# First attention: the context's turns of two batches ahead, issued ahead of the first two heads' scores

## The chip, the cores and the metric

The kernel runs on one core of one Trainium2 chip. The metric is device microseconds of one execution, the median of several runs. In the profile PE is TensorE (matrix products and transposes), PEld its weight loads, DVE is VectorE, ACT is ScalarE, POOL is GpSimd and SP is the engine that issues most DMAs. Each engine runs its own list of instructions strictly in order; engines meet only at semaphores.

## The reference, cut to what matters

The network has four layers, each an attention over a context and a mixture of experts, with gated residuals. Data are float32: x is 16 batches x 100 tokens x 256, the context 16 x 361 x 192. The change is in the first layer's attention, which per batch computes

```
xn = layernorm(ctx, ln_x_g, ln_x_b)                   # 361 x 192
ln = layernorm(layernorm(x), ln_l_g, ln_l_b)          # 100 x 256
q  = ln @ Wq.T
k, v = concat([xn @ Wkv.T, ln @ Wlkv.T], axis=1) split in two
q, k normalized by their root mean square per head (4 heads of 64)
attn = softmax(mask(q @ k.T)) ; out = (attn @ v) @ Wo.T + bo
x = x + tanh(g_xattn[0]) * out
```

so the keys are 361 of the context and 100 of the tokens, padded to 512 columns. Expert layers and three more attentions follow and are the same in both kernels.

## The kernel before, in words

The program is written engine by engine, its order by hand, with counting semaphores. The first attention treats one batch t at a time and works on three batches at once: while batch t is attended, the projections of t + 1 are finished and those of t + 2 begun. `three_deep` (line 218) runs batches 0 to 3 unrolled, 4 to 11 as two rounds of a loop of four, and 12 to 15 unrolled.

Each batch has twelve numbered steps on TensorE, each filling one of two banks of PSUM in turn (`J_bank`), which another engine empties; a step may begin when the step before the last has been copied out (line 2370 or 2344: `wait_for(pe, s.copied, order_of(t, n) - 1)`). The steps in their order are `AHEAD = (0, 1, 5, 6, 2, 8, 3, 4, 9, 10, 7, 11)`:

- 0 and 1, `ctx_turn` (line 2379): three 128 x 128 transposes each of the normalized context of batch t + 2; ScalarE copies each out with gain and bias (line 1067) into CT.
- 5 and 6, then 7 and 11, in pairs: the projections of the context to keys and values. 192 rows of contraction are taken as 128 (`pair_blocks`, line 2352) and 64 (`pair_rests`, line 2360); the two rests of a pair use the two halves of TensorE's rows. ScalarE squares and copies the results out (lines 1075 to 1077, 1079, 1080, 1082).
- 2, 3 and 4: the turn of the tokens (line 2396, copied at line 1071), queries, and keys and values of the tokens (both line 2402).
- 8, 9 and 10: the turns of the normalized keys and queries of batch t + 1 (lines 2419 and 2422), copied out by ScalarE (lines 1087 and 1089).

TensorE's attention proper: `scores` (line 2468, two heads at a time, each in one half of the rows, into banks 0 and 1), `probs_turn` (line 2479), `weigh` (line 2500), `o_turn` (line 2509, with a transpose for the router, line 2281) and `project` (line 2519). VectorE adds the mask to the scores and takes the maximum (line 1605), negates it (line 1609) and copies turned probabilities out (line 1620). ScalarE takes the exponential (line 1112), which waits for the maximum.

VectorE's order within a batch (line 1750): maxima of heads 0 and 1; a sum of squares for t + 1; statistics of the context and tokens of t + 3; probabilities of heads 0 and 1; the context's norm; maxima of heads 2 and 3; residual, router, sums of squares for t + 2; probabilities of heads 2 and 3; the scaling of the output. ScalarE's order (line 1180): copies of steps 7 and 11 of t + 1; copies of steps 0 and 1 of t + 2; exponentials of heads 0 and 1; the copy of the output; copies of 5, 6 and 2; exponentials of heads 2 and 3; copies of 8, 3, 4, 9 and 10.

On TensorE the bank of step 0 of batch t + 2 was last filled by step 7 of batch t + 1, that of step 1 by step 11; both come from the rests that open the batch:

Of the kernel before, what the change touches and what calls it, by code (L numbers as in the profile page):

```python
# [136 lines left out]
def order_of(t, n):  # L137

    if n not in OF_NEXT:
        return ALONE.index(n) if isinstance(t, int) and t == 0 else 9 + 12 * (t - 1) + AHEAD.index(n)  # L140
    return 9 + 12 * t + (n - 8 if isinstance(t, int) and t == B - 1 else AHEAD.index(n))
# [24 lines left out]
def copied_by(L, t):  # L166

    return STEPS[L] if L == 1 and isinstance(t, int) and t == 0 else VALUE_PAIRS[L][-1][0]
# [7 lines left out]
def follows(t, by):  # L176

    return not isinstance(t, int) or t + by < B
# [7 lines left out]
def wait_for(eng, signal, count):  # L186

    if isinstance(count, int) and count <= 0:
        return
    eng.wait_ge(signal.sem, signal.before + count)  # L190
# [48 lines left out]
def flamingo_kernel(nc, a, out):  # L239
    ctx = ExitStack()  # L240
    with ctx:
# [313 lines left out]
        def kt(L, j):  # L555
            m = 4 if L == 1 else 2
            return KT[j][:, 0:m * 512].rearrange("p (m n) -> p m n", m=m)
# [1716 lines left out]
        def _(pe):  # L2274
# [31 lines left out]
            def attention(L):  # L2306
# [11 lines left out]
                def part_of(t, j, n, r, rest):  # L2318

                    c = 1 - r if rest else r  # L2320
                    lo, hi = (REST * c, REST * (c + 1)) if rest else (0, P)
                    if L == 0:
                        keys = (r if n in FIRST_PAIRS[0] else 2) * P
                        cols = slice(0, 512) if n in FIRST_PAIRS[0] else slice(D * r, D * (r + 1))
                        return ((J_bank[parity_of(t, n)][:, 0:cols.stop - cols.start], CT[j][lo:hi, c, keys:keys + P],
                                 wkv0[lo:hi, c, cols]),)
                    dst = step_bank(L, t, j, n)
                    if n in sum(KEY_PAIRS[L], ()):
                        m = sum(KEY_PAIRS[L], ()).index(n)
                        return ((dst[:, 0:NC], wk[L][lo:hi, c, m * P:(m + 1) * P], CT[j][lo:hi, c, 0:NC]),)  # L2330
                    last = CT[j][lo:hi, c, 2 * P:3 * P]
                    if L == 1 and n >= 8:
                        return ((dst[:, 0:256], last, wv[1][lo:hi, c, 256 * r:256 * (r + 1)]),)
                    whole = (dst[:, 0:VN], CT[j][lo:hi, c, r * P:(r + 1) * P], wv[L][lo:hi, c, 0:VN])
                    if L == 1:
                        return (whole,)
                    return (whole, (dst[:, 256:384], last, wv[2][lo:hi, c, P * r:P * (r + 1)]))

                def pair_blocks(t, j, pair):

                    for r, n in enumerate(pair):
                        if L == 0:

                            wait_for(pe, s.copied, order_of(t, n) - 1)
                            if n == 5:
                                wait_for(pe, s.copied, order_of(t, 1) + 1)
                        else:
                            wait_for(pe, s.copied, STEPS[L] * t + place_of(L, t, n) - 1)
                            if n == KEY_PAIRS[L][0][0]:
                                wait_for(pe, (s.ctx_in0, s.ctx_in1)[j], 32 * (t // 2 + 1))  # L2350
                        for i, (to, lhs, rhs) in enumerate(part_of(t, j, n, r, False)):
                            nc.tensor.matmul(to, lhs, rhs, start=(i == 0), stop=False, skip_group_check=True)  # L2352

                def pair_rests(t, j, pair):

                    parts = [part_of(t, j, n, r, True) for r, n in enumerate(pair)]
                    for i in range(len(parts[0])):
                        for r in range(2):
                            to, lhs, rhs = parts[r][i]
                            ins = nc.tensor.matmul(to, lhs, rhs, start=False, stop=True, skip_group_check=True)  # L2360
                            if i == len(parts[0]) - 1:
                                ins.then_inc(s.proj.sem, 1)
# [82 lines left out]
                def scores(t, j, h):  # L2445
                    n = H * t + h
                    k = (H * j + h) % 2

                    if PAIRS[L] == 0:
                        wait_for(pe, s.exped, n - 1)  # L2450
                    elif h % 2 == 0:
                        wait_for(pe, s.exped, n)
                    if h == 0 and L == 0:

                        wait_for(pe, s.copied, order_of(t, 10) + 1)
                    elif h == 0 and L == 3:

                        wait_for(pe, s.copied, STEPS[L] * (t + 1))
                    elif h == 0:

                        wait_for(pe, s.copied, STEPS[L] * t + copied_by(L, t))
                    if H == 1:
                        for c, m in ((0, CW[0]), (1, CW[1] + 1)):
                            ins = nc.tensor.matmul(S_bank[k][0:T, 0:NK], QT[j][0:m, c, :], CT[j][0:m, c, 0:NK],
                                                   start=(c == 0), stop=(c == 1))
                    else:
                        m, b = h // 2, W * (h % 2)
                        ins = nc.tensor.matmul(S_bank[k][0:T, 0:NK], QT[j][b:b + W, m, :], kt(L, j)[b:b + W, m, 0:NK],  # L2468
                                               start=True, stop=True)
                    ins.then_inc(s.scores.sem, 1)  # L2470
# [32 lines left out]
                def o_turn(t, j, slot=0):  # L2503

                    wait_for(pe, s.o_scaled, 2 * (t + 1))
                    wait_for(pe, s.resid, 2 * t)
                    for m in range(H * W // P):
                        n, lo = (CW[m], m * HALF) if L == 3 else (P, m * P)
                        ins = nc.tensor.transpose(R_bank[0:n, m * T:(m + 1) * T], O[0:T, lo:lo + n], ident[0:T, 0:T])
                    if L == 0 and not (isinstance(t, int) and t == 0):  # L2510
                        ins = router_turn(t - 1, slot)
                    ins.then_inc(s.o_turned.sem, 1)
# [93 lines left out]
                def ahead(t, q, steps):  # L2606

                    for n in steps:
                        if n not in OF_NEXT and follows(t, 2):
                            step(t + 2, (q + 2) % 4, n)  # L2610
                        if n in OF_NEXT and follows(t, 1):
                            step(t + 1, (q + 1) % 4, n)

                def first_attend(t, q):
                    j = q % 2
                    started = not (isinstance(t, int) and t == 0)
                    if follows(t, 1):
                        pair_rests(t + 1, 1 - j, FIRST_PAIRS[1])
                    scores(t, j, 0)
                    scores(t, j, 1)  # L2620
                    ahead(t, q, (0, 1))
                    if started:
                        o_turn(t - 1, 1 - j, (q + 2) % RING)
                    if follows(t, 2):
                        pair_blocks(t + 2, j, FIRST_PAIRS[0])
                    probs_turn(t, j, 0)
                    probs_turn(t, j, 1)
                    if follows(t, 2):
                        pair_rests(t + 2, j, FIRST_PAIRS[0])
                    scores(t, j, 2)  # L2630
                    scores(t, j, 3)
                    if started:
                        project(t - 1, 1 - j)
                    ahead(t, q, (2,))
                    weigh(t, q, 0)
                    weigh(t, q, 1)
                    ahead(t, q, (8, 3, 4, 9, 10))
                    if follows(t, 2):
                        pair_blocks(t + 2, j, FIRST_PAIRS[1])
                    probs_turn(t, j, 2)  # L2640
                    probs_turn(t, j, 3)
                    weigh(t, q, 2)
                    weigh(t, q, 3)
# [487 lines left out]
```

## Time and profile before

| | |
|---|---|
| runs | 1673.85, 1675.27, 1681.13 us; median 1675.27 |
| profiled execution | 1673.62 us, span 1671.4 us |
| busy, share of the span | PE 91%, PEld 66%, DVE 54%, ACT 36%, POOL 17% |
| first attention, batch 7 (182.7 to 202.8 us) | PE 18.17, DVE 15.60, ACT 10.78, POOL 11.52 us |
| granted TensorE clock, mean | 0.952 |

A batch is taken here from the start of its first scores to that of the next batch's. Times of the timeline count from the start of the span. A row gives the start, the time taken, engine, line, operation, output and input with their shapes and the number of instructions merged into it; what stands in brackets at its end is the idle time of the engine before it and what ended that. An engine's consecutive rows can overlap by some tenths of a microsecond, since a new instruction enters before the last is out. A float32 matrix product shows as two records, a transpose as one.

### The profile page before, as it was taken

How to read it: one execution, taken by the hardware profiler on the slowest of the kernel's cores; microseconds unless marked ns; L12 is line 12 of the kernel's file. 1: busy time of each engine (PE TensorE's matmuls, PEld its weight loads, DVE VectorE, ACT ScalarE, POOL GpSimd, SP SyncE). 2: the span in 40 equal slices, each digit the busy share in tenths (PEclk: the TensorE clock that was granted, in tenths of full speed). 3: DMA queues.
4: the chain of work that ended last, by engine and by line, in shares of the span. 5: the costliest groups of instructions: out<-in, count | busy, mean ns of one | idle time of the engine just before them, and what ended most of it. 6: DMA issues, size and time to landing. Idle time of an engine off the chain costs nothing.

```text
span 1671.4 us, 30315 instructions
## 1 busy us (share of the span) xinstructions
PE 1515.2 (91%) x9070; PEld 1100.3 (66%) x9070; DVE 900.9 (54%) x2901; ACT 607.6 (36%) x1705; POOL 291.3 (17%) x409
## 2 busy tenths in 40 slices
PE   5889889878999989999999989979999899787986
PEld 2555555557999966777677666747777644565664
DVE  4678787652222224555444444556665555565665
ACT  3555555512333223344443424314444100444422
POOL 4555555411000031000000000110000011121000
PEclk8999999958999989999999989989999799999888
DMA  5011112618999940000000000011010100342000
GB/s 135 16 45 37 36 34 62 200 44 281 332 327 327 330 151 22 19 18 18 18 15 11 9 1 10 16 41 37 27 35 18 32 16 19 85 149 66 1 20 20
DMA packets 89654, 128.85 MB, mean 77 GB/s; under 512 B 17362, under 2 KB 74786, under 8 KB 84450
## 3 DMA queue, kind: packets, MB, share of 16 engines
q1 hardware_dynamic: 85954, 123.50, 22.9%
q0 software_dynamic: 2432, 4.34, 0.8%
q8 instruction: 39, 0.64, 0.2%
q14 instruction: 45, 0.37, 0.1%
q10 hardware_dynamic: 1184, 0.01, 0.0%
HBM read 112.87 MB, written 11.67 MB: 75 GB/s over the span
## 4 chain that ended last, share of the span: by engine, by line
PE 70%; issue 10%; DVE 8%; POOL 6%; ACT 3%; DMA 1%; POOLq 0%; ACTq 0%; SPq 0%; DVEq 0%
PE bank L2352 9%; PE bank L2706 8%; PE bank L2500 8%; PE bank L2799 5%; PE bank L2360 5%; PE bank L2468 4%; PE bank L2720 4%; PE bank L2519 4%; PE bank L2752 3%; PE bank L2479 3%; PE bank L2768 3%; PE bank L2441 2%; POOL work L922 2%; PE bank L2952 2%; DVE work L1620 1%
## 5 line engine op out<-in xcount | busy, mean ns | idle before, releaser
L1620 DVE COPY work<-bank 128x300 f32<-128x300 f32 (+1 forms) x272 | 123.2, 490 | 178.6 <-PE bank L2479 177.3
L2500 PE MATMUL bank<-work 128*100 128x64 f32 (+1 forms) x1760 | 193.7, 261 | 19.3 <-DVE work L1620 17.4
L2500 PEld LDWEIGHTS bank<-work 128*100 128x100 f32 x1760 | 175.2, 171 | 47.5 <-DVE work L1620 28.3
L1112 ACT ACTIVATE work<-bank,work 100x361 f32<-100x361 f32 (+1 forms) x272 | 158.7, 590 | 49.4 <-DVE work L1611 34.8
L2706 PE MATMUL bank<-work 128*128 128x128 f32 x1216 | 142.2, 275 | 0.0
L1955 DVE SCALAR_TENSOR_TENSOR work<-bank,work 128x128 f32<-128x128 f32 x160 | 56.2, 351 | 158.9 <-PE bank L2706 148.1
L2706 PEld LDWEIGHTS bank<-work 128*128 128x128 f32 x1216 | 140.4, 192 | 1.0
L1611 DVE TENSOR_REDUCE work<-bank 100x1 f32<-100x361 f32 x208 | 101.9, 528 | 69.3 <-PE bank L2468 66.7
L2479 PEld LDWEIGHTS bank<-ident,work 100*128 100x128 f32 x880 | 92.1, 144 | 42.1 <-issue 22.7
L2479 PE MATMUL bank<-ident,work 100*128 100x100 f32 x880 | 103.9, 254 | 7.3 <-ACT work L1112 7.0
L1233 ACT ACTIVATE work<-bank,work 128x128 f32<-128x128 f32 x160 | 58.7, 367 | 142.2 <-PE bank L2706 137.2
L2468 PE MATMUL bank<-work 64*100 64x361 f32 (+1 forms) x512 | 109.0, 503 | 0.6 <-ACT work L1096 0.6
L1102 ACT COPY work<-bank 128x512 f32<-128x512 f32 (+2 forms) x96 | 41.3, 482 | 166.5 <-PE bank L2360 166.5
L900 POOL TENSOR_TENSOR work<-work,neg_half 100x1 f32<-100x1 f32 x64 | 35.2, 550 | 340.1 <-DVE work L1569 305.3
L922 POOL TENSOR_TENSOR work<-work,neg_half 128x4 f32<-128x4 f32 x80 | 82.0, 1025 | 65.1 <-DVE work L1593 65.1
L2799 PE MATMUL bank<-F_weight,work 128*128 128x512 f32 (+1 forms) x208 | 92.4, 603 | 0.0
L859 POOL TENSOR_TENSOR work<-work,neg_half 100x1 f32<-100x1 f32 x48 | 28.1, 586 | 296.5 <-DVE work L1477 271.0
L1099 ACT COPY work<-bank 128x361 f32<-128x361 f32 x96 | 39.6, 465 | 94.6 <-PE bank L2360 94.6
L2720 PE MATMUL bank<-work 128*128 128x256 f32 x320 | 72.5, 380 | 0.5 <-DVE work L1955 0.5
L2799 PEld LDWEIGHTS bank<-F_weight,work 128*128 128x128 f32 (+1 forms) x208 | 39.1, 190 | 49.2 <-issue 39.8
L2352 PE MATMUL bank<-L_WkvT,work 128*128 128x512 f32 (+1 forms) x128 | 52.9, 536 | 17.3 <-ACT work L1067 13.8
L2720 PEld LDWEIGHTS bank<-work 128*128 128x128 f32 x320 | 59.3, 190 | 7.9 <-DVE work L1955 0.7
(343 smaller groups left out, 2770.4 us busy)
## 6 DMA issues: line engine op xcount, KB each, us to landing
work<-in_F_w SPq DMA_DIRECT2D x58, 1024.0 KB, 5.8
work<-in_ctxT SPq DMA_DIRECT2D x64, 180.5 KB, 2.3
work<-context_norms SPq DMA_DIRECT2D x32, 288.0 KB, 3.4
context_norms<-work SPq DMA_DIRECT2D x16, 288.0 KB, 2.5
work<-in_ctx SPq DMA_DIRECT2D x16, 192.0 KB, 2.6
work<-in_F_b SPq DMA_DIRECT2D x20, 128.0 KB, 6.1
work<-sorted_x SPq DMA_DIRECT2D x20, 128.0 KB, 2.2
sorted_y<-work SPq DMA_DIRECT2D x20, 128.0 KB, 5.7
```

What stands on the lines that cost most here:

```text
L922: nc.gpsimd.tensor_tensor(rr[j][:, 4 * k:4 * k + 4], rr[j][:, 4 * k:4 * k + 4], neg_half[:, 0:4], ALU.pow).then_inc(s.rqk.sem, 1)
L1112: nc.scalar.activation(pr[:, 0:NK], S_bank[k][0:T, 0:NK], ACT.Exp, bias=nmax[k][0:T, :], accum_out=rsum[j][0:T, h:h + 1]).then_inc(s.exped ...
L1611: nc.vector.tensor_reduce(nmax[k][0:T, :], S_bank[k][0:T, 0:NK], axis=AXX, op=ALU.max, negate=True).then_inc(s.maxed.sem, 1)
L1620: nc.vector.tensor_copy(PT[k][:, 0:CH, :], PT_bank[k][:, 0:CH * T].rearrange("p (c t) -> p c t", c=CH)).then_inc(s.probs_copied.sem, 1)
L2352: nc.tensor.matmul(to, lhs, rhs, start=(i == 0), stop=False, skip_group_check=True)
L2360: ins = nc.tensor.matmul(to, lhs, rhs, start=False, stop=True, skip_group_check=True)
L2468: ins = nc.tensor.matmul(S_bank[k][0:T, 0:NK], QT[j][b:b + W, m, :], kt(L, j)[b:b + W, m, 0:NK], start=True, stop=True)
L2479: ins = nc.tensor.transpose(PT_bank[k][:, c * T:(c + 1) * T], PR[k][0:T, c, :], ident[0:T, 0:T])
L2500: ins = nc.tensor.matmul(to, PT[k][:, c, :], values, start=(c == 0), stop=(c == CH - 1))
L2706: ins = nc.tensor.matmul(bank[to + f % 2][:, 0:P], first_weights(i, j)[:, c, col:col + P], TT[j][:, c, :], start=(c == 0), stop=(c == 1))
L2720: ins = nc.tensor.matmul(bank[6 + j][:, 0:D], AC[j][:, f, :], W2[j][:, f, :], start=(f == 0), stop=(f == HID0 // P - 1))
L2799: ins = nc.tensor.matmul(bank[3 + q % Y_BANKS][0:k, :], GXT[:, c, i * P:i * P + k], lin2[:, c, 2 * g:2 * g + 2, :].rearrange("p e n -> p ( ...
```

## The change

In TensorE's list for the first attention, the call that issues steps 0 and 1 of batch t + 2 moves ahead of the scores of heads 0 and 1. It acts in batches 0 to 13; batches 14 and 15 have no batch two ahead. Other engines' lists, all waits and all operands stay.

```
@@ first_attend(t, q), TensorE
                     if follows(t, 1):
                         pair_rests(t + 1, 1 - j, FIRST_PAIRS[1])
+                    ahead(t, q, (0, 1))
                     scores(t, j, 0)
                     scores(t, j, 1)
-                    ahead(t, q, (0, 1))
                     if started:
                         o_turn(t - 1, 1 - j, (q + 2) % RING)
                     if follows(t, 2):
```

## Rows read from the trace of the kernel before

**Rows 1.** Busy time in stretches: window, length, busy us of each engine, clock, DMA
```profile
182.70:202.80 20.10, 18.17 (x116) 12.11 (x114) 15.60 (x62) 10.78 (x30) 11.52 (x15) 1.00 0.12 37
202.80:225.00 22.20, 18.57 (x116) 12.05 (x114) 15.98 (x62) 11.11 (x30) 9.92 (x13) 1.00 0.11 33
183.90:192.80 8.90, 8.25 (x54) 5.46 (x54) 8.37 (x30) 5.33 (x15) 3.79 (x5) 1.00 0.21 63
```

**Rows 2.** Waits, 50 to 300 us: who, for whom, total us, times, longest
```profile
PE bank L2352 <- ACT work L1067: 8.4, 12, 0.9
```

**Rows 3.** Timeline, TensorE, batch 7: start, us, line, work, idle before
```profile
182.16 0.70 PE L2360 MATMUL bank<-L_WkvT,work 64*128 64x256 f32 x4
182.69 1.02 PE L2468 MATMUL bank<-work 64*100 64x512 f32 x4
183.75 0.87 PE L2390 MATMUL bank<-ident,work 128*128 128x128 f32 x6
185.61 1.98 PE L2352 MATMUL bank<-L_WkvT,work 128*128 128x512 f32 x4 [0.65 <-ACT work L1067]
187.44 0.85 PE L2479 MATMUL bank<-ident,work 100*128 100x100 f32 x8
194.91 1.98 PE L2402 MATMUL bank<-L_WlkvT,work 128*128 128x512 f32 x4
202.80 1.02 PE L2468 MATMUL bank<-work 64*100 64x512 f32 x4
```

**Rows 4.** Timeline, ScalarE, batch 7
```profile
183.25 0.37 ACT L1080 COPY work<-bank 128x256 f32<-128x256 f32 x1
184.33 1.23 ACT L1067 ACTIVATE work<-bank,L_ln_x_b,L_ln_x_g 128x384 f32<-128x384 f32 x2 [0.43 <-PE bank L2390]
193.49 0.69 ACT L1112 ACTIVATE work<-bank,work 100x512 f32<-100x512 f32 x1
194.16 0.70 ACT L1087 ACTIVATE work<-bank,L_kn_g 128x512 f32<-128x512 f32 x1
```

**Rows 5.** Timeline, VectorE, batch 7
```profile
183.90 0.70 DVE L1605 CUSTOM_DVE_ANT_0 bank<-bank,work 100x512 f32<-100x512 f32 x1 [0.99 <-PE bank L2468]
192.63 0.15 DVE L1609 TENSOR_SCALAR work<-work 100x1 f32<-100x1 f32 x1
```

**Rows 6.** Timeline, batch 7: weight loads of the turns; rests behind transposes
```profile
183.74 0.64 PEld L2390 LDWEIGHTS bank<-ident,work 128*128 128x128 f32 x6 [0.88 <-issue]
188.22 1.13 PE L2360 MATMUL bank<-L_WkvT,work 64*128 64x512 f32 x4
```

**Rows 7.** Timeline, batch 8, which begins VectorE's second round of its loop
```profile
206.69 0.70 DVE L1605 CUSTOM_DVE_ANT_0 bank<-bank,work 100x512 f32<-100x512 f32 x1 [3.68 <-issue]
209.50 0.56 PE L2479 MATMUL bank<-ident,work 100*128 100x100 f32 x4 [0.29 <-ACT work L1112]
217.14 1.98 PE L2402 MATMUL bank<-L_WlkvT,work 128*128 128x512 f32 x4 [0.53 <-ACT work L1087]
```

**Rows 8.** Timeline, batches 0 and 3: fourth maximum's negation, exponential of head 3
```profile
54.05 0.15 DVE L1609 TENSOR_SCALAR work<-work 100x1 f32<-100x1 f32 x1
54.24 0.69 ACT L1112 ACTIVATE work<-bank,work 100x512 f32<-100x512 f32 x1
112.00 0.15 DVE L1609 TENSOR_SCALAR work<-work 100x1 f32<-100x1 f32 x1
113.10 0.69 ACT L1112 ACTIVATE work<-bank,work 100x512 f32<-100x512 f32 x1
```

**Rows 9.** Batch 14: busy time in a stretch; timeline of TensorE
```profile
325.00:345.00 20.00, 17.08 (x94) 12.38 (x92) 11.58 (x44) 6.52 (x16) 4.05 (x5) 0.74 0.04 10
328.36 0.56 PE L2479 MATMUL bank<-ident,work 100*128 100x100 f32 x4 [1.49 <-ACT work L1112]
329.27 0.56 PE L2479 MATMUL bank<-ident,work 100*128 100x100 f32 x4 [0.35 <-ACT work L1112]
329.76 1.47 PE L2468 MATMUL bank<-work 64*100 64x512 f32 x4
```

More of the change, by code:

```diff
@@ L2618, in first_attend @@
                         pair_rests(t + 1, 1 - j, FIRST_PAIRS[1])
+                    ahead(t, q, (0, 1))
                     scores(t, j, 0)
                     scores(t, j, 1)
-                    ahead(t, q, (0, 1))
                     if started:
```

## The prediction

> **What bounds the kernel now.** The change touches only the first attention (44 to 360 us of the span), so I read that stage: stretches of busy time first, then the waits, then one batch instruction by instruction on each engine. The reader is to see, first, that batch 7 takes 20.1 us, of which TensorE is busy 18.2, VectorE 15.6, ScalarE 10.8 and GpSimd 11.5, at the full clock [rows 1]. (The page's chain runs through GpSimd here and mostly says "issue"; an engine idle for half of the batch that waits on VectorE's results is no bound, so I don't follow it.) TensorE is the bound, with short stalls. One of them is the target: the blocks of keys (line 2352) wait for ScalarE's copies of the turned context (line 1067), 12 times between 50 and 300 us, 8.4 us in total [rows 2].
>
> Second, what TensorE does before that stall [rows 3]. The rests end at 182.86 (182.16 + 0.70), the two scores run from 182.69 to 183.71, the six turns start at 183.75 and take 0.87, the blocks start at 185.61 after 0.65 idle. The turns could not have started much earlier: the first goes into the bank that step 7 filled, and ScalarE's copy of it ends at 183.62 [rows 4]. The scores lie in exactly that hole.
>
> Third, and this decides for me: VectorE begins its batch with the maxima of those scores, at 183.90, and between 183.90 and 192.80 it is busy 8.37 of 8.90 us [rows 1, 5]. It has no slack from the first maximum to the fourth. Behind the fourth stand, on ScalarE, the exponentials of heads 2 and 3 and then the copy of step 8 (line 1087, ends 194.86), and TensorE's step 4 starts at 194.91, when that copy frees its bank [rows 3, 4].
>
> **The change part by part.** Nothing is added or removed: in each of batches 0 to 13 six transposes pass two score matmuls (batches 14 and 15 have no context two ahead). No DMA and no other engine's order changes; ScalarE already copies the turns before its exponentials. TensorE takes the waits along, so the scores, the turn of the output, the blocks and all behind now queue behind the turns' wait.
>
> (a) The turns' wait. The copy of step 7 ends at 183.62; from ScalarE's end to TensorE's start pass 0.05 (185.56 to 185.61) [rows 3, 4], so the turns start at 183.67 instead of 183.75 (the last three wait for step 11 in the same way, whose copy follows at once). TensorE, with nothing to do in between, idles 0.81 from the end of the rests. This is new cost, since its cover, the scores, is gone.
>
> (b) The scores. Turns until 183.67 + 0.87 = 184.54, scores 1.02, end 185.56 instead of 183.71: 1.85 us later. Bounds: 1.78 if the scores overlap the turns' tail by the 0.07 by which line 2360 overlaps the transposes before it, and 1.97 if they take the 1.13 which that row of four 512-column matmuls takes behind transposes [rows 6]; I take 1.85, which is between.
>
> (c) The stall at the blocks. The copies of the context come 0.08 earlier, but the scores and then 0.34 of turns of the output (184.62 to 184.96) stand first: the blocks start at 185.56 + 0.34 = 185.90, without a stall. The 0.65 is filled by 1.02 of scores, after a new hole of 0.81: TensorE alone loses 0.29 a batch.
>
> (d) What is late next on TensorE: the turn of the second head's probabilities. In the batch where VectorE started late, it began 2.81 us behind the first maximum (206.69 to 209.50) [rows 7]. With the maximum at 183.90 + 1.85 = 185.75 that is 188.56, against 187.44 + half of 0.85 = 187.87 now: 0.69 late, which contains the 0.29.
>
> (e) What is late next through VectorE: its first maximum is 1.85 late and nothing up to the fourth absorbs it. The only slack is ScalarE's: the fourth maximum's negation ends at 192.78, the exponential of head 3 starts at 193.49 although 0.04 would do: 0.67. So exponential, copy of step 8 and step 4 come 1.85 - 0.67 = 1.18 late, which contains the 0.69 of (d). Batch 8 is a trial of this: VectorE came back from its loop 2.68 us late (206.69 against 183.90 + 20.11, without any wait for another engine), and step 4 started at 217.14 instead of 194.91 + 20.11 = 215.02, 2.12 late [rows 3, 5, 7]: 0.56 absorbed, near the 0.67. Behind step 4 all waits up to the next rests are between TensorE and ScalarE and shift along, VectorE is idle 4.5 us in a batch, so it catches up before the next maxima. GpSimd gets its sums 1.85 later; it is idle 8.6 of 20.1 [rows 1].
>
> (f) The sum. ScalarE's slack, read as in (e) for each batch, is 0 in batch 0, 0.18, 0.50 and 0.91 in batches 1 to 3, 0.48, 0.60, 0.59, 0.67 in 4 to 7, 0.58, 0.59, 0.67 in 9 to 11, 0.86 in 12 and 1.25 in 13 (two of the pairs in [rows 8]). Batches 0 to 3: 7.40 - 1.59 = 5.8. Batches 4 to 7 and 9 to 11: 12.95 - 4.18 = 8.8. Batch 12: 1.0. Batch 13: 0.7, by (d), since its slack leaves less. Batch 8: 0, for there VectorE's return (206.69) is later than the new scores (202.80 + 1.02 + 1.85 + the 0.19 from scores to maximum = 205.86). Sum: +16.3 us. The next stage starts behind the last batch and shifts whole. The profiled execution took 1673.62 (span 1671.4); with the sum 1689.9. The median of the runs is 1.65 higher, so 1690 to 1691.5.
>
> A rule that speaks against the change: loading of the turns' weights starts only at 183.74, 0.88 after the loads before, when the half-row scores are through; but in the other direction, line 2360 starts at once behind the transposes [rows 6]. The Trainium skill, TensorEngine Tiling (Array Packing), Key Properties, says that changing the tiling mode drains the engine. The change makes one change of mode per batch (rests and scores to turns) into three. By the row a drain shows no gap in a matmul's start, so I add 0; by the page two more drains a batch would be charged, which makes the kernel slower still.
>
> **The rivals.**
> 1. *TensorE's loss only.* VectorE's delay is absorbed ahead of step 4. Then the loss is the 0.29 of (c) to the 0.69 of (d), in 12 batches (0 and 8 have longer stalls there): 3.5 to 8.3 us, about 1680. For it: VectorE does have 4.5 us idle in a batch. Against it: none of that lies between the first and fourth maximum, and batch 8 handed on 2.12 of 2.68.
> 2. *The stall goes, and little takes its place: faster.* If TensorE is the only bound and the turns' new wait is under 0.65, the two scores fill the old stall. It decides at a hole of 0.65 between rests and turns; with half of my 0.81 the gain is 0.25 in 13 batches, 3 us: 1672; with none 8.5 us, 1667. It needs ScalarE to copy step 7 sooner, and that copy starts from the rests, which don't move; and it needs VectorE not to matter.
> 3. *The clock falls.* In batch 14, after idling 1.49 before a turn of probabilities and 0.35 before the next, TensorE's granted clock fell, 0.74 on average from 325 to 345, and two scores then took 1.47 instead of 1.02 [rows 9]. The Trainium skill, TensorE: Matmul & The Clock Gate, Part 1, says that throttled is the default and activity releases it. The change makes stalls of 0.81, some 0.3 and 0.5 a batch. Against it: batch 8 with 18.57 busy of 22.2 stayed at 1.00 [rows 1], as much as I expect of the changed batches. At half clock two scores cost 0.45 more; a dip in every batch over both pairs of scores and as much work again costs some 2 us each (an estimate from these rows), 26 us on top of my sum, 1716; a few dips give 1695.
>
> That the change doesn't do what it says is excluded: the order on TensorE is written by hand, and the bank's wait moves along.
>
> **How the numbers follow.** My forecast 0.74, rival 1 0.14, rival 2 0.05, rival 3 0.07. Time 1690. The forecast's own range comes from (b), 1.78 to 1.97 in 12 batches (-1 to +1.4), ScalarE's slack off by 0.15 each (2 us) and the runs' spread: 1685 to 1696. The range takes in the upper part of rival 1 and the small dips of rival 3: 1681 to 1697. 0.5% is 8.4 us, about what a measurement can tell from no change: rival 1 lies within it but for its top, rival 2 also, but for its end near 1667. Faster 0.03, same 0.15, slower 0.82.
>
> **What would show it.** Right: the turns start some 0.05 after the end of line 1080, with TensorE idle 0.8 before them; no stall before line 2352; the first maximum 2.9 after the end of the rests instead of 1.04; step 4 waiting for line 1087 in every batch; batches of 21.3 us, and batch 8 near 22.2 as before. Wrong: batches of 20.4 to 20.8 would say that VectorE's delay is absorbed (rival 1), a hole under 0.65 rival 2, a granted clock under 1 before 325 us rival 3.

## The result, and the profile after

The changed kernel is slower. Over the first four executions its median is 1696.18 us (1687.33 to 1697.98) against 1674.91 before (1673.85 to 1681.13): a ratio of 1.0109, 95% interval 1.0066 to 1.0152. Five more rounds on another occasion gave 1.0102 (1.0072 to 1.0131). The forecast was 1690, range 1681 to 1697. The profiled execution of the changed kernel took 1697.98 us, span 1695.8, mean granted clock 0.952 as before.

First the stage as a whole. A mark that both kernels pass in the same way is ScalarE's square of step 7 (line 1079), 0.11 us behind the rests that open a batch. In the timeline of the kernel before, its first row is that of batch 0 and its second that of batch 14:

```profile
44.65 0.38 ACT L1079 ACTIVATE work<-bank 128x256 f32<-128x256 f32 x1 [1.42 <-PE bank L2360]
...
325.54 0.38 ACT L1079 ACTIVATE work<-bank 128x256 f32<-128x256 f32 x1 [4.16 <-PE bank L2360]
```

That is 280.89 us for 14 batches; in the changed kernel it is 342.63 - 44.76 = 297.87 (first and last row of the second fence below). So the stage is 16.98 us longer; the sum had said 16.3.

Busy time in stretches of the changed kernel, with the columns of [rows 1]: batch 7, batch 8, from the first to the fourth maximum of batch 7, and the 20 us with the least TensorE work of the stage.

```profile
192.70:214.06 21.36, 18.60 (x114) 11.90 (x114) 15.49 (x61) 11.09 (x30) 11.41 (x16) 1.00 0.12 35
214.07:236.82 22.75, 18.69 (x114) 11.89 (x114) 16.00 (x61) 11.12 (x30) 10.66 (x14) 1.00 0.12 32
195.56:204.45 8.89, 8.69 (x59) 5.71 (x58) 8.35 (x30) 5.21 (x15) 3.03 (x4) 1.00 0.05 13
205.00:225.00 20.00, 15.97 (x90) 9.30 (x89) 12.89 (x51) 9.06 (x26) 11.22 (x14) 1.00 0.13 37
```

Batch 7 takes 21.36 us instead of 20.1, with the busy time of every engine unchanged within 0.5 us [rows 1]: TensorE idles 0.83 us more and is busy 0.43 more, most of which is scores of 1.10 instead of 1.02 and eight transposes in two groups (0.56 and 0.57) instead of one run of 0.85. VectorE is again busy 8.35 of 8.89 us between first and fourth maximum. The clock stays at 1.00, also where TensorE is busy only 15.97 of 20.

The timeline of the changed kernel, all engines, batch 7 with marks of batches 0, 8 and 14. Answering rows of before: line by line in [rows 3 to 5], for 218.20 to 228.65 in [rows 7].

```profile
44.76 0.39 ACT L1079 ACTIVATE work<-bank 128x256 f32<-128x256 f32 x1 [1.43 <-PE bank L2360]
...
191.90 0.70 PE L2360 MATMUL bank<-L_WkvT,work 64*128 64x256 f32 x4
...
192.99 0.37 ACT L1080 COPY work<-bank 128x256 f32<-128x256 f32 x1
...
193.49 0.87 PE L2390 MATMUL bank<-ident,work 128*128 128x128 f32 x6 [0.89 <-ACT work L1080]
...
194.07 1.23 ACT L1067 ACTIVATE work<-bank,L_ln_x_b,L_ln_x_g 128x384 f32<-128x384 f32 x2 [0.43 <-PE bank L2390]
194.29 1.10 PE L2468 MATMUL bank<-work 64*100 64x512 f32 x4
...
195.56 0.70 DVE L1605 CUSTOM_DVE_ANT_0 bank<-bank,work 100x512 f32<-100x512 f32 x1 [2.92 <-PE bank L2468]
195.72 1.91 PE L2352 MATMUL bank<-L_WkvT,work 128*128 128x512 f32 x4
...
198.29 0.57 PE L2479 MATMUL bank<-ident,work 100*128 100x100 f32 x4 [0.20 <-ACT work L1112]
...
204.29 0.15 DVE L1609 TENSOR_SCALAR work<-work 100x1 f32<-100x1 f32 x1
...
204.48 0.69 ACT L1112 ACTIVATE work<-bank,work 100x512 f32<-100x512 f32 x1 [0.22 <-DVE work L1609]
205.16 0.68 ACT L1087 ACTIVATE work<-bank,L_kn_g 128x512 f32<-128x512 f32 x1
...
205.89 1.98 PE L2402 MATMUL bank<-L_WlkvT,work 128*128 128x512 f32 x4 [0.50 <-ACT work L1087]
...
218.20 0.70 DVE L1605 CUSTOM_DVE_ANT_0 bank<-bank,work 100x512 f32<-100x512 f32 x1 [4.21 <-issue]
...
221.02 0.56 PE L2479 MATMUL bank<-ident,work 100*128 100x100 f32 x4 [0.29 <-ACT work L1112]
...
228.65 1.98 PE L2402 MATMUL bank<-L_WlkvT,work 128*128 128x512 f32 x4 [0.53 <-ACT work L1087]
...
342.63 0.39 ACT L1079 ACTIVATE work<-bank 128x256 f32<-128x256 f32 x1 [4.16 <-PE bank L2360]
```

The rests end at 192.60 and the turns start at 193.49: a hole of 0.89, and its row names ScalarE's copy of step 7 as what ended it. The scores come behind, take 1.10 instead of 1.02, and VectorE's first maximum starts at 195.56, 2.96 behind the rests' end instead of 1.04. The blocks (195.72) have no stall any more. But step 4 (205.89) stalls 0.50 for the copy of step 8, which stands behind the exponential of head 3, which waits 0.22 for the fourth negation. The waits of the changed kernel from 50 to 315 us (us in total, times, longest) show the exchange:

```profile
DVE bank L1605 <- PE bank L2468: 31.6, 11, 3.0
...
PE bank L2390 <- ACT work L1080: 10.0, 12, 0.9
...
PE bank L2402 <- ACT work L1087: 7.7, 13, 1.6
```

The row of [rows 2], line 2352 for line 1067, is gone; in its place TensorE waits 10.0 us for line 1080 in 12 turns, and 7.7 for line 1087 in 13. VectorE now waits 31.6 us for scores in 11 turns; from 50 to 300 us of the kernel before it waited 11.0 in 11.

The stretch behind the stage differs from execution to execution. From the mark in batch 14 to the end of the execution it was 1348.1 us before, 1355.4 in the changed kernel's first profile and 1348.6 in its second; in the seven other profiles of this study it lay between 1343 and 1353. The 7 us by which the first profile exceeds 1673.62 + 16.98 lie there, and the second profile of the same kernel doesn't have them, so I don't count them as the change's.

### The profile page after: what moved, and what is told of

Read it like the earlier page. It is cut to its first block, busy times and chain, and to the rows that moved or that the text cites. A ratio compares the mean times of both kernels' runs of the same rounds, so it can differ in the third digit from the quotient of the medians.

```text
span 1695.8 us, 30315 instructions
## 1 busy us (share of the span) xinstructions
PE 1522.4 (90%) x9070; PEld 1097.6 (65%) x9070; DVE 898.4 (53%) x2901; ACT 612.0 (36%) x1705; POOL 291.5 (17%) x409
## 4 chain that ended last, share of the span: by engine, by line
PE 67%; issue 12%; DVE 9%; POOL 6%; ACT 3%; DMA 2%; POOLq 0%; SPq 0%; ACTq 0%; DVEq 0%
PE bank L2352 8%; PE bank L2500 8%; PE bank L2706 7%; PE bank L2799 5%; PE bank L2360 5%; PE bank L2468 4%; PE bank L2720 4%; PE bank L2519 4%; PE bank L2752 3%; PE bank L2479 3%; PE bank L2768 3%; POOL work L922 2%; PE bank L2441 2%; PE bank L2952 2%; DVE work L1620 1%
## 5 line engine op out<-in xcount | busy, mean ns | idle before, releaser
L1605 DVE CUSTOM_DVE_ANT_0 bank<-bank,work 100x512 f32<-100x512 f32 x64 | 44.7, 698 | 48.6 <-PE bank L2468 43.7
```

## The experiments

"Stage" is the time from line 1079's start in batch 0 to that in batch 14. The changed kernel, profiled twice, gave it within half a microsecond, while the timed runs of the kernel before spread from 1664.7 to 1681.1; so the stage is read first.

| | stage, us | against before | plain batch (7), us | ratio to before, 95% interval |
|---|---|---|---|---|
| before | 280.89 | | 20.11 | |
| changed | 297.87 | +16.98 | 21.36 | 1.0109 (1.0066 to 1.0152) |
| changed, again | 297.39 | +16.50 | 21.36 | 1.0102 (1.0072 to 1.0131) |
| copy of step 8 first | 288.61 | +7.72 | 20.77 | 1.0047 (1.0027 to 1.0066) |
| statistics first | 294.74 | +13.85 | 20.93 | 1.0065 (1.0043 to 1.0086) |
| one turn moved | 294.35 | +13.46 | 21.07 | 1.0063 (1.0040 to 1.0086) |
| before, copy of step 8 first | 277.98 | -2.91 | 19.95 | 0.9990 (0.9971 to 1.0009) |
| changed, no square of step 7 | 293.70 | +12.81 | 21.08 | 1.0053 (1.0023 to 1.0082) |
| before, block after copy 0 | 274.45 | -6.44 | 19.54 | 0.9935 (0.9905 to 0.9964) |
| before, block and copy of step 8 | 270.26 | -10.63 | 19.39 | 0.9926 (0.9897 to 0.9955) |

**1. Is it VectorE's late maximum, by way of the copy of step 8?** In the changed kernel, on ScalarE:

```
                     ahead(t, q, (5, 6, 2, 8))
                     exp(t, j, 2)
                     exp(t, j, 3)
-                    ahead(t, q, (8, 3, 4, 9, 10))
+                    ahead(t, q, (3, 4, 9, 10))
```

(the 8 of the first line is added there.)

> The changed kernel, and on ScalarE the copy of step 8 moves ahead of the exponentials of heads 2 and 3 (before the change and in it, it stands behind them). The stage is measured from the start of line 1079 in batch 0 to its start in batch 14: 280.9 us before, 297.9 with the change. Theory (VectorE's late fourth maximum holds back ScalarE's copy of step 8 and by it TensorE's step 4): the copy no longer waits for a maximum, so a plain batch keeps only what TensorE itself is late at line 2396, 0.82 instead of 1.24 to 1.8; batch 0 about 0.3, batch 8 about 0; stage 291, 7 us less than with the change, time 1685 to 1689. Rival (TensorE's hole and the drains between tiling modes carry all of it, VectorE does not matter): stage 297 to 298, no gain over the change.

Measured: stage 288.61, below the 291 expected; the median time, 1679.2, is below the 1685 to 1689 expected. The timeline of batch 7 in this kernel:

```profile
187.85 0.70 DVE L1605 CUSTOM_DVE_ANT_0 bank<-bank,work 100x512 f32<-100x512 f32 x1 [2.92 <-PE bank L2468]
...
196.58 0.15 DVE L1609 TENSOR_SCALAR work<-work 100x1 f32<-100x1 f32 x1
...
196.86 0.69 ACT L1087 ACTIVATE work<-bank,L_kn_g 128x512 f32<-128x512 f32 x1 [1.07 <-PE bank L2419]
...
197.60 1.98 PE L2402 MATMUL bank<-L_WlkvT,work 128*128 128x512 f32 x4
...
198.11 0.69 ACT L1112 ACTIVATE work<-bank,work 100x512 f32<-100x512 f32 x1
```

The first maximum is as late as in the changed kernel (2.85 behind the mark at 185.00), the fourth negation ends at 196.73, and the copy of step 8 no longer waits for it: step 4 follows at 197.60 without a stall, 12.60 behind the mark, against 13.18 with the change and 11.94 before. The rival, no gain, is out. 9.3 of the 17.0 us hung on that copy's place.

**2. The control: the same edit in the kernel before.**

> Control: the kernel before, with only ScalarE's copy of step 8 ahead of the exponentials of heads 2 and 3. Theory: in plain batches step 4 was held back by that copy by under 0.1, so almost nothing; batch 0 gains about 0.5 and batch 8 about 0.5. Stage 279.3 to 280.3, time the same as before within 0.2%. If it gained as much as the first experiment does against the change (7 us), the theory's path would not be the one that the change lengthened.

Measured: 277.98, a gain of 2.91, of which 0.56 in batch 0, 0.49 in batch 8 and 0.14 to 0.16 in each other batch. It is more than the 0.6 to 1.6 expected: step 4 was held back by 0.16 in plain batches, not by under 0.1. So of the 9.3 us of experiment 1, 2.9 are the edit's own. If the edit is worth the same in both, the rest, 6.4, is what the change lost through the fourth maximum; 10.6 (288.61 - 277.98) is what remains when step 4 is free of it.

**3. VectorE from the other side.** In the changed kernel, VectorE's list:

```
+                    if follows(t, 3):
+                        ln_ctx_stats(t + 3, 1 - j)
                     maximum(t, j, 0)
                     maximum(t, j, 1)
...
                     if follows(t, 3):
-                        ln_ctx_stats(t + 3, 1 - j)
                         ln_x(t + 3, 1 - j)
```

> The changed kernel, and VectorE takes the context's statistics of batch t + 3 (1.85 us, lines 1537 to 1543, which need no scores) ahead of the maxima of heads 0 and 1 instead of behind them. Theory: they fit into VectorE's wait for the late scores (2.9 us), the first maximum starts as with the change (2.8 to 2.9 after line 1079's start), the fourth is 1.85 earlier, about where it was before the change, and plain batches lose only TensorE's 0.82; batch 8, where VectorE comes late out of its loop, loses 2 to 2.5 more than before, because the statistics now push its first maximum back. Stage 292 to 294. Rival (VectorE does not matter): 297 to 298, plain batches stay at 21.4.

Measured: stage 294.74, slightly above 292 to 294. VectorE in batches 7 and 8 of this kernel (mark of batch 7 at 186.73):

```profile
186.58 0.87 DVE L1537 BATCH_NORM_STATS2 work<-work 128x6 f32<-128x192 f32 x3
...
189.58 0.70 DVE L1605 CUSTOM_DVE_ANT_0 bank<-bank,work 100x512 f32<-100x512 f32 x1 [1.51 <-PE bank L2469]
...
197.52 0.15 DVE L1609 TENSOR_SCALAR work<-work 100x1 f32<-100x1 f32 x1
...
211.59 0.88 DVE L1537 BATCH_NORM_STATS2 work<-work 128x6 f32<-128x192 f32 x3 [4.00 <-issue]
```

The statistics run in the wait for the scores, the first maximum is where the change has it (2.85 behind the mark), and the fourth negation ends at 197.67, 10.94 behind the mark instead of the 11.73 of the changed kernel. That is 0.79 earlier and not 1.85: here the statistics take only 1.49 (to 188.07), and VectorE then waits 0.91 for GpSimd at the context's norm, which it had not done before. Even so, the plain batches (4 to 7 and 9 to 11) lose 0.82 to 0.97 instead of 1.25 to 1.45. Batch 8 loses 3.04 where 2 to 2.5 were expected: VectorE came back from its loop after 4.00 and had the statistics still to do. So VectorE's order matters, with the same TensorE list; the rival is out a second time.

**4. Half of the change.** `ahead(t, q, (0,))` before the scores, `ahead(t, q, (1,))` behind them:

> Only half of the change: step 0 (three transposes) goes ahead of the scores, step 1 stays behind them. Theory: the same hole of 0.8 before the first turn, the scores end 0.43 earlier than with the change, so VectorE's first maximum is 1.49 late instead of 1.92 and step 4 is 1.49 less ScalarE's slack of about 0.6, some 0.9 late; the stall at line 2352 is back (0.4 to 0.8 us), since the second context copy comes later. Plain batches 21.0, stage 293 to 294. Rival (drains between tiling modes): this order has four changes of mode instead of three, so the stage would not fall below 297.

Measured: stage 294.35, slightly above the 293 to 294 expected, batch 7 21.07 (mark at 188.55):

```profile
189.33 0.54 PE L2390 MATMUL bank<-ident,work 128*128 128x128 f32 x3 [0.88 <-ACT work L1080]
189.80 1.11 PE L2468 MATMUL bank<-work 64*100 64x512 f32 x4
...
191.08 0.70 DVE L1605 CUSTOM_DVE_ANT_0 bank<-bank,work 100x512 f32<-100x512 f32 x1 [2.59 <-PE bank L2468]
...
192.15 1.98 PE L2352 MATMUL bank<-L_WkvT,work 128*128 128x512 f32 x4 [0.42 <-ACT work L1067]
```

The hole is the same (0.88), VectorE's maximum starts 0.32 earlier behind the mark than with the change (expected 0.43: three transposes alone take 0.54, not half of 0.87), and a stall of 0.42 is back at the blocks. The stage is 3.5 us shorter than with the change. Its rival is not tested by this, though: the expectation counts four changes of tiling mode (work on half of TensorE's rows, as rests and scores, against work on all, as transposes), but rests, turns, scores, turns, turns of the output are three changes, as many as in the change. What it shows is that with the same number of changes the loss falls by 3.5 us. The drains are weighed below, in the section on the prediction.

**5. The hole by itself.** Step 7's square is left out of the changed kernel in batches 1 to 15:

```
                         elif n == 7:
-                            nc.scalar.square(QKsq[:, 2, :], src[:, 0:D])
+                            if isinstance(t, int) and t == 0:
+                                nc.scalar.square(QKsq[:, 2, :], src[:, 0:D])
                             ins = nc.scalar.copy(QK[j][:, 2, :], src[:, 0:D])
```

> The changed kernel without ScalarE's square of step 7 (line 1079) in batches 1 to 15, so that part of the keys is normalized with the sum of squares of batch 0; all else is as in the change. It shortens by 0.28 what the first turn waits for. Theory (the hole between rests and turns is ScalarE's copying of step 7, and it is passed on through VectorE in full): turns, scores and first maximum 0.26 to 0.28 earlier, plain batches 0.26 to 0.28 shorter than with the change, 3.4 to 3.6 us over batches 0 to 7 and 9 to 13; the time from line 1080's start in batch 0 to that in batch 14 is 294.2 to 294.6 instead of 297.9. Rival (the turns wait for the draining array, not for the copy): unchanged, 297.5 to 298.

Measured, between the starts of step 7's copy: 293.70 against 297.87 and 297.39 in the two profiles of the change. Batch 7 in this kernel (the copy is line 1081, the turns line 2391):

```profile
190.17 0.70 PE L2361 MATMUL bank<-L_WkvT,work 64*128 64x256 f32 x4
...
190.97 0.37 ACT L1081 COPY work<-bank 128x256 f32<-128x256 f32 x1 [4.23 <-PE bank L2361]
...
191.47 0.87 PE L2391 MATMUL bank<-ident,work 128*128 128x128 f32 x6 [0.61 <-ACT work L1081]
```

The rests end at 190.87, the turns start at 191.47: the hole is 0.60 instead of 0.89, and each batch but batch 8 is 0.27 to 0.32 shorter, 3.7 us in all against the second profile. (The range expected, 294.2 to 294.6, was reckoned from the first profile, whose batch 8 was 0.5 longer.) So a shorter hole is returned in full.

**6. The change again.**

> The changed kernel again, beside the next three on one chip, with five rounds, because the timed loss (+21 us by the medians) was larger than the +17.0 us of the stage in the profile, and what follows the stage took 7 us longer in that profile. Theory: the stage (line 1079's start in batch 0 to that in batch 14) takes 297.9 us again within 0.5, against 280.9 before, and what comes after it varies by some us from execution to execution in every kernel; the ratio to the kernel before is 1.010 to 1.011. Rival (the change also lengthens the later stages): what follows the stage is again 5 us or more longer than in the kernel before, and the ratio is 1.013.

Measured: stage 297.39, ratio 1.0102, what follows the stage 1348.6. What follows the stage is 0.5 us longer than in the kernel before and not 5, so the rival, longer later stages, is out. Batch 8 alone is 0.51 shorter than in the first profile (22.24 instead of 22.75), all of the 0.48 by which the stages differ.

**7. The stall met in another way.** In the kernel before, `pair_blocks` (TensorE):

```
                             wait_for(pe, s.copied, order_of(t, n) - 1)
-                            if n == 5:
-                                wait_for(pe, s.copied, order_of(t, 1) + 1)
```

> The kernel before (scores ahead of the turns), and the first block of line 2352 (step 5) no longer waits for the copies of both turns: the extra wait for step 1's copy is taken out, since that block reads only step 0's half of the context; the second block still waits for step 1's copy through its bank. So the target of the change, the stall of 0.65 at line 2352, is met without moving the scores. Theory: the blocks start 0.6 earlier in each batch, and this is worth at step 4 what VectorE's fourth maximum allows, ScalarE's slack of 0 to 0.9: about 7 us; stage 273.5 to 275, time 0.4% less than before. Rival (a stall filled here comes back at the turn of the probabilities): stage 280 to 281.

Measured: 274.45. The gain is 0 in batch 0, 0.02 in batch 8, 0.19 and 0.52 in batches 1 and 2, 0.49 to 0.63 in the others. In batch 7:

```profile
175.77 0.38 ACT L1079 ACTIVATE work<-bank 128x256 f32<-128x256 f32 x1 [4.24 <-PE bank L2358]
...
177.12 1.23 ACT L1067 ACTIVATE work<-bank,L_ln_x_b,L_ln_x_g 128x384 f32<-128x384 f32 x2 [0.43 <-PE bank L2388]
...
177.85 1.98 PE L2350 MATMUL bank<-L_WkvT,work 128*128 128x512 f32 x4
```

The blocks start 2.08 behind the mark instead of 2.64, in the middle of ScalarE's two copies (line 1067). This gain is what the change was after, and in batches 0, 1, 2 and 4 it ends at the slack of (f): 0, 0.18, 0.50 and 0.48 there, 0, 0.19, 0.52 and 0.49 measured.

**8. Both edits on the kernel before.**

> The kernel before with both: the first block of line 2352 waits for step 0's copy alone, and ScalarE's copy of step 8 goes ahead of the exponentials of heads 2 and 3. Theory: step 4 no longer depends on VectorE's fourth maximum, so the whole 0.65 of each batch is kept, and the 2.9 us of the control come on top: stage 269 to 271, time 0.6% to 0.7% less than before. If VectorE bounds the batch elsewhere (its probabilities for heads 2 and 3), the two gains do not add and the stage stays at 272 to 274.

Measured: 270.26; the two gains, 6.44 and 2.91, add to 9.35 and the pair gives 10.63. Of the 1.28 more, 0.63 lie in batch 0 (1.19 instead of 0.56 and 0) and 0.43 in batch 1 (0.77 instead of 0.15 and 0.19), the batches in which ScalarE's slack of 0 and 0.18 had held back the edit of experiment 7 alone. The stage by its marks:

```profile
41.32 0.38 ACT L1079 ACTIVATE work<-bank 128x256 f32<-128x256 f32 x1 [1.43 <-PE bank L2358]
...
311.58 0.38 ACT L1079 ACTIVATE work<-bank 128x256 f32<-128x256 f32 x1 [4.16 <-PE bank L2358]
```

This version beats both kernels: 0.9926 (0.9897 to 0.9955) of the time before, 1659.68 us by the median against 1672.35 on the same occasion.

## Why the prediction was right

Step by step, batch 7 where nothing else is said, times behind the mark of line 1079 (182.97 before, 192.71 after):

| step | forecast | measured |
|---|---|---|
| (a) turns' start, hole | 0.70, 0.81 | 0.78, 0.89 |
| (b) first maximum later by | 1.85 (1.78 to 1.97) | 1.92 (0.93 to 2.85) |
| (c) blocks later by | 0.29 | 0.37 |
| (d) second turn of probabilities later by | 0.69 | 0.68 |
| (e) step 4 later by | 1.18 | 1.24 |
| (f) batch 8 | 0 | 0.52, in the second profile 0.01 |
| (f) batch 13 | 0.7 | 0.73 |
| (f) sum over the stage | 16.3 | 16.98 and 16.50 |

The mechanism and nearly all of its sizes hold, and batch by batch too. The first maximum is 1.92 to 1.94 later in the batches of the loop (4 to 7, 9 to 11) and 1.77 to 1.80 later in the unrolled ones (0 to 3, 12), all inside the bounds of (b); less the slack of (f), this is the measured loss of each of these twelve batches within 0.03. (The upper bound, 1.97, should read 1.96: 1.85 and the 0.11 from 1.02 to 1.13.)

Two terms were a little off. In (a) I took 0.05 from the end of ScalarE's copy to TensorE's start; in batch 7 it is 0.13 (193.36 to 193.49), and the turns begin no earlier behind the mark than before. The kernel before shows the same 0.13 (183.62 to 183.75, [rows 3, 4]) and experiment 5 too (191.34 to 191.47), so in batch 7 it had already been waiting for that copy and not for the scores, also where the prediction reads the late weight loads of the turns as waiting for the scores; its scores cost nothing there at all, and the hole is 0.08 larger than forecast. In the unrolled batches the 0.05 holds and the hole is 0.08 smaller than forecast; batch 1 of the changed kernel:

```profile
65.83 0.37 ACT L1080 COPY work<-bank 128x256 f32<-128x256 f32 x1
...
66.25 0.89 PE L2390 MATMUL bank<-ident,work 128*128 128x128 f32 x6 [0.73 <-ACT work L1080]
```

There the copy ends at 66.20. Why the hand-over is longer in the loop is not shown. The two errors, some 0.08 a batch upward in seven batches and downward in five, nearly cancel in the sum; that part of its accuracy is luck. In (b) the scores behind transposes take 1.10 where they took 1.02 behind the rests [rows 3]; the bound of 1.13 was nearer than my value.

The Trainium skill's TensorEngine Tiling (Array Packing), Key Properties, has a drain at each change of tiling mode. No run measured the drain alone, but the rows bound it. In batch 7, from the end of the rests to the end of the blocks, TensorE takes 4.73 before (182.86 to 187.59), of which it idles 0.65 and 0.04 [rows 3], and 5.03 with the change (192.60 to 197.63), of which it idles 0.89: the same work takes 4.04 and 4.14, with two more changes of mode. The same sum gives 0.2 in the unrolled batches and 0.3 in batch 0. So drains are worth at most some 2 us of the 17 (an estimate from these rows), and (b) had most of that already, since it charged the scores their full 1.02 although they had ended only 0.85 behind the rests (182.86 to 183.71).

Step (d) hides a detail: the second turn of probabilities was 0.68 late as forecast, but the next rests 0.82 (6.07 against 5.25), because eight transposes in two groups of 0.56 and 0.57 take longer than in one run of 0.85. That lies under step 4's 1.24 and costs nothing in the change; it is what keeps experiment 1 at 0.82 at the tokens' turn and not at 0.69.

Rival 1 (TensorE's loss only) fell: step 4 waits for line 1087 in each of batches 0 to 12, and experiments 1 to 3 moved the time by editing ScalarE and VectorE alone. Its loss is a part, though, and larger than the 3.5 to 8.3 us that I gave it: 10.6 us lie between the kernels of experiments 1 and 2, in both of which the fourth maximum no longer counts, 0.68 to 1.06 in each batch but batch 8, where I gave 0.29 to 0.69. Rival 2 (faster) fell with the hole: 0.89, or 0.73 in the unrolled batches, against the 0.65 from which it would have decided. Rival 3 (the clock) fell: 1.00 throughout the stage. Its price was read too low: the 1.47 of two scores in batch 14 [rows 9] is a row during which the clock fell (0.69 from 330 to 331 us, 0.50 from 331 to 334), and at 0.50, the lower of the two levels, the next row, line 2519, took 2.03 instead of the 1.11 of batch 7. The forecast's time, 1690, is near the second median, 1689.7. The first, 1696.2, is just above the 1685 to 1696 that I gave the forecast itself and within 1 us of the end of the whole range; its profiled execution contains 7 us from behind the stage, which the prediction had no term for.

## What to carry to other kernels

Work that fills a wait can't be moved out of it without asking what else waits for that work: here the two score matmuls covered ScalarE's copying at next to no cost, and VectorE, which has no slack for half of the batch, began with their result. Read the slack where the chain ends (the exponential that starts 0.67 after its maximum), not from an engine's share of busy time; VectorE had 4.5 us idle per batch and passed the delay on all the same. And before reordering around a stall, look at what the stalled instruction really reads: of the two copies that the block waited for, it needed one, and 0.56 of its 0.65 us were for the other.

## What was not expected

VectorE's return at the end of its loop varies: it idles 3.68 us in the kernel before and in the second profile of the change, 4.21 in the first, and 4.00, 3.75 and 3.70 in experiments 3, 4 and 2. It is the whole difference between the two profiles' batch 8 (0.52 and 0.01). No experiment here shortened it, and its cause is not shown.

The rest of the program, 1343 to 1355 us behind the stage, varied by more than half of what the change did. Some of that goes with the granted clock, which is 1.00 in the stage and 0.94 or 0.95 behind it in the profile of before and the two of the change: of the 31 runs of the kernel before beside experiments 1 to 4, the eight with a mean clock of 0.950 to 0.954 took 1673.1 to 1680.6 us, the nine with 0.959 to 0.962 took 1665.2 to 1671.6. In a kernel of this length a change of one per cent is sized by the stretch that it touches, profile against profile.
